# A feed-forward's products with half of the layer stack put between them, and its weights kept split in DRAM

## The reference, cut to what matters

```python
x = x + _L0_attn_a_ref(_layernorm(x), ...)     # stack: DEPTH 4, DIM 64, DFF 256
x = x + _L0_ffn_ref(_layernorm(x), ...)        # I = 1792, w_eff = w * (su @ sv), rank 4
x = x + _L0_attn_b_ref(_layernorm(x), ...)
x = x + _L0_ffn_ref(_layernorm(x), ...)
...
# the stack: project to 64 features, then four times
y = silu(layernorm(h)); y = sconv(y); h = h + y * scl      # sconv: a complex recurrence over 256 tokens
y = layernorm(h); y = silu(y @ w1.T + b1); h = h + (y @ w2.T + b2)
# then layernorm, and a product back to 512 features
```

## Time and profile before

| | us |
|---|---|
| median of 3 runs | 2623.54 (2622.83 to 2625.76) |
| the profiled execution | 2625.9 |
| its span | 2624.2 |
| PE busy | 2521.0 (96%) |
| DVE busy | 1533.0 (58%) |
| ACT busy | 1056.4 (40%) |
| POOL busy | 657.9 (25%) |

### The profile page before, as it was taken

The page is one execution under the profiler, slowest core; times in us unless marked ns, Lnnn a source line. Parts: engine busy times, 40 slices in busy tenths (PEclk is TensorE's granted clock), DMA queues, the critical chain, the costliest instruction groups (busy, mean ns, idle before and its releaser), DMA issues.

```text
span 2624.2 us, 38718 instructions
## 1 busy us (share of the span) xinstructions
PE 2521.0 (96%) x13406; PEld 2141.7 (82%) x13406; DVE 1533.0 (58%) x3579; ACT 1056.4 (40%) x2692; POOL 657.9 (25%) x1156
## 2 busy tenths in 40 slices
PE   3888999999989999999999999999999989999999
PEld 3564788888868888888888888888888868888887
DVE  6776655454446666666666666666666655445443
ACT  2221233333325454544545445545444433333332
POOL 6442000000013343443433434434343310000000
PEclk8767899999989999999999999999999989999999
DMA  3000343222210010000000100001000002323231
GB/s 116 1 0 25 120 169 121 97 97 96 97 42 25 1 41 1 17 25 1 25 18 1 41 1 17 25 1 41 1 17 25 1 29 101 115 87 112 96 112 65
DMA packets 29840, 132.87 MB, mean 51 GB/s; under 512 B 4744, under 2 KB 4872, under 8 KB 29648
## 3 DMA queue, kind: packets, MB, share of 16 engines
q1 hardware_dynamic: 27472, 128.95, 14.5%
q10 hardware_dynamic: 2176, 1.45, 0.2%
HBM read 115.18 MB, written 15.20 MB: 50 GB/s over the span
## 4 chain that ended last, share of the span: by engine, by line
PE 91%; DVE 4%; issue 2%; POOL 1%; ACT 1%; DMA 0%; SPq 0%; DVEq 0%; ACTq 0%; POOLq 0%
PE psum L298 81%; PE psum L1346 3%; PE psum L1321 2%; PE psum L874 1%; PE psum L782 1%; POOL srstd L432 1%; PE psum L883 1%; PE psum L864 1%; PE psum L1301 1%; DVE ln_bn L552 1%; PE psum L773 0%; DVE buf_c L701 0%; PE psum L849 0%; DMA x<-in_x 0%; PE psum L1283 0%
## 5 line engine op out<-in xcount | busy, mean ns | idle before, releaser
L298 PE MATMUL psum<-wkvq_h,axT_h 128*128 128x256 f32 (+1 forms) x1024 | 358.3, 350 | 1.5 <-DVE axT_l L1192 1.5
L298 PE MATMUL psum<-wkvq_h,axT_l 128*128 128x256 f32 (+1 forms) x1024 | 346.8, 339 | 0.0
L298 PE MATMUL psum<-wkvq_l,axT_h 128*128 128x256 f32 (+1 forms) x1024 | 346.3, 338 | 0.0
L1169 POOL TENSOR_SCALAR prob<-prob,rsum 128x128 f32<-128x128 f32 (+1 forms) x512 | 212.7, 428 | 445.0 <-DVE rsum L1261 436.6
L1114 ACT ACTIVATE prob<-biased,nmax 128x128 f32<-128x128 f32 (+1 forms) x512 | 226.2, 443 | 216.2 <-DVE nmax L1254 216.2
L298 PEld LDWEIGHTS psum<-wkvq_h,axT_l 128*128 128x128 f32 x1024 | 195.4, 191 | 21.8
L298 PE MATMUL psum<-wo_h,oT_h 128*128 128x512 f32 x512 | 212.7, 415 | 0.0
L298 PEld LDWEIGHTS psum<-wkvq_h,axT_h 128*128 128x128 f32 x1024 | 195.7, 191 | 17.8 <-issue 1.9
L298 PEld LDWEIGHTS psum<-wkvq_l,axT_h 128*128 128x128 f32 x1024 | 196.1, 191 | 16.1
L298 PE MATMUL psum<-wo_h,oT_l 128*128 128x512 f32 x512 | 201.7, 394 | 0.0
L298 PE MATMUL psum<-wo_l,oT_h 128*128 128x512 f32 x512 | 200.6, 392 | 0.0
(11 more groups left out here) (374 smaller groups left out, 6501.7 us busy)
## 6 DMA issues: line engine op xcount, KB each, us to landing
stage<-weff_dram SPq DMA_DIRECT2D x66, 768.0 KB, 4.2
raw2b<-weff_dram SPq DMA_DIRECT2D x18, 768.0 KB, 4.2
stage<-in_wqkv SPq DMA_DIRECT2D x16, 768.0 KB, 4.3
raw2a<-weff_dram SPq DMA_DIRECT2D x14, 768.0 KB, 4.2
stage<-in_wo SPq DMA_DIRECT2D x16, 512.0 KB, 4.0
stage<-in_ffn_w SPq DMA_DIRECT2D x9, 768.0 KB, 5.5
weff_dram<-stage SPq DMA_DIRECT2D x9, 768.0 KB, 4.0
x<-in_x SPq DMA_DIRECT2D x4, 1024.0 KB, 13.4
```

The costliest lines, as they stand in the source:

```text
L298: ins = pe.matmul(out_ap, stat[a], mov[b], start=start and n == 0, stop=stop and n == last)
L1169: pool.tensor_scalar(prob[:, b, lo:hi], prob[:, b, lo:hi], rsum[:, b, t:t + 1], 1.0, ALU.mult, ALU.mult).then_inc(prob_done, 1)
```

## The change

- **The stack is cut in two.** Blocks 0 and 1 run first, side by side, block 1 later than block 0 by 15 us of a table of step times (`STEP_US`). Block 2 begins one chunk behind the start of the feed-forward, block 3 behind 15 chunks; their steps stand in the lists between the feed-forward's. A `gate`, `up` or `down` is issued in two halves of 6 matmuls, and a stack step can stand between the halves. `merged` puts the chains together by their planned times; a chunk counts as 9.6 us, and a step of blocks 2 and 3 as 1.15 times its table entry, plus 0.8 us if it has work for PE.
- **Buffers and banks.** The stack has two sets of buffers instead of four. Block 0 has two PSUM banks of its own; blocks 1 to 3 share the two banks of `scale` and `fxT` (`AUX`), and PE waits before each use until the last but one user has left (`wait_bank`).
- **The weights are stored in both parts.** In token block 0 they are scaled and split as before, and both parts go to DRAM (`save`), 1.5 MB per chunk. In blocks 1 to 3 and in the second feed-forward, `load` brings both parts back, and nothing is split. Raw weights have two buffers (`stage`), the split ones three (`WSLOTS`). One chunk of the second feed-forward is loaded at the end of the attention, where two raw ones were.
- **The start.** `rstd` of block 0's first norm stands ahead of the last `table` step on POOL.

```diff
+WSLOTS = 3
+
+STEP_US = {"row": 0.6, "xT": 1.6, "proj": 3.6, "h0": 0.6, "cen": 0.8, "sq": 0.5, "var": 0.6, "rstd": 1.6, "rexp": 1.0,
+           "rtr": 0.6, "yn": 0.5, "silu": 0.8, "rot": 0.9, "scan": 1.9, "res": 1.2, "aff": 0.5, "w1": 1.1, "hid": 1.5,
+           "w2": 1.9, "hm": 0.6, "out": 0.5, "xadd": 0.7}
...
-        hres = [sb(f"h{i}", [P, SW], F32, phase1) for i in range(NS)]
...
+        SETS = 2
...
+        hres = [sb1(f"h{i}", [P, SW]) for i in range(SETS)]
+        buf_a, buf_b, buf_c, buf_d, buf_e = ([sb1(f"buf_{n}{i}", [P, SW]) for i in range(SETS)] for n in "abcde")
+        hidden = sb1("hidden", [P, SETS, FC, NG2 * SW])
...
+            d["wgu"] = [place(where if s else head, f"wgu{s}{tag}", [P, 2, 2 * DM], F32R) for s in range(WSLOTS)]
+            d["wdn"] = [place(where if s else head, f"wdn{s}{tag}", [P, 2, DM], F32R) for s in range(WSLOTS)]
...
+        STACK_XT = (0, 1, 1, 0)
+
+
+        LAG = 15.0
+        HALF = 1.6
+        CHUNK = 6 * HALF
...
+        def stack_chain(s, start, busy_from):
+
+            at, chain = start, []
+            for name, n in STACK:
+                chain.append((at, (name, s, n)))
+                at += STEP_US[name] * (1.0 if at < busy_from else 1.15)
+                if at >= busy_from and (name, n) in ON_PE:
+                    at += 0.8
+            return chain, at
...
+                    fresh_next = p == 0 and n + 1 < IC
+                    early, mid, late = [], [], []
+                    if fresh_next:
+                        early, mid = [("scale", n + 1, 0)], [("scale", n + 1, 1), ("sgu", n + 1, 0)]
+                        late = [("scale", n + 1, 2), ("sdn", n + 1, 0)]
                     if n + 2 < NBLK * IC:
-                        order.append(("fetch", n + 2, 0))
-                    elif n + 2 == NBLK * IC and p == 0:
-                        order.append(("kvq", 0, 0))
...
+                    chain += [(t + 2 * HALF, ("up", n, 0)), (t + 3 * HALF, ("up", n, 1))]
+                    chain += [(t + 3 * HALF, e) for e in late]
...
+                        chain += [(t + 4 * HALF, ("down", n - 1, 0)), (t + 5 * HALF, ("down", n - 1, 1))]
...
+        def merged(chains):
+
+
+            order, nxt, holders = [], [0] * len(chains), []
+            while any(k < len(chain) for k, chain in zip(nxt, chains)):
...
+        chain0, ready = stack_chain(0, 0.0, 1e9)
+        first_prep = [(ready + 0.6 * k, e) for k, e in enumerate(
+            [e for step in norm_prep(0, 0) for e in step])]
+        ffn_at = ready + 9.0
...
+        set_up = [(0.5 + 2.5 * k, ("table", k + 1, 0)) for k in range(7)]
+        set_up += [(6.0 + k, ("lr", k, 0)) for k in range(4)]
+        set_up += [(12.0, ("fetch", 0, 0)), (12.0, ("fetch", 1, 0))]
...
+        first_weights = [(ready - 8.0 + 2 * k, e) for k, e in enumerate(
+            [("scale", 0, 0), ("scale", 0, 1), ("sgu", 0, 0), ("scale", 0, 2), ("sdn", 0, 0)])]
+        order1 = merged([chain0, stack_chain(1, LAG, ffn_at)[0], set_up, norms, first_weights, first_prep,
+                         ffn_chain(0, ffn_at, [("kvq", 0, 0)]),
+                         stack_chain(2, ffn_at + CHUNK, 0.0)[0],
+                         stack_chain(3, ffn_at + (IC + 1) * CHUNK, 0.0)[0]])
+        order3 = [("load", 1, 1)] + prep_steps(0) + merged([ffn_chain(1, 0.0, [])])
...
+        GATE, UP, DOWN, AUX = 0, 1, 2, (6, 7)
+        OWN = (2, 3)
...
+        def wait_bank(e):
+
+            first = aux_at[e]
+            for n in range(first, first + (NG2 if e[1] == "w1" else 1)):
+                if n < 2:
+                    continue
+                p, what, a, b = aux_use[n - 2]
+                if what in ("scale", "fxT"):
+                    pe.wait_ge(aux_free, aux_freed[p, what, a, b])
+                elif what == "w1":
+                    pe.wait_ge(stk_act[a], ON_ACT["hid", b, FC - 1])
+                else:
+                    left = {"xT": ("xlo", b), "proj": ("h0", b), "cen": ("cenc", b), "var": ("eps", b), "rtr": ("yn", b),
...
+        def save(n):
+
+            sp.wait_ge(gu_lo, n + 1)
+            sp.dma_start(weff_gu[n], F1["wgu"][n % WSLOTS][:].bitcast(F32)).then_inc(gu_out[n % WSLOTS], 16)
+            sp.wait_ge(dn_lo, n + 1)
+            sp.dma_start(weff_dn[n], F1["wdn"][n % WSLOTS][:].bitcast(F32)).then_inc(dn_out[n % WSLOTS], 16)
...
+            for out_sem, in_sem, used, src, key in ((gu_out, gu_in, up_mm, weff_gu, "wgu"),
+                                                    (dn_out, dn_in, dn_mm, weff_dn, "wdn")):
+                if p == 0 and T == 1:
+                    sp.wait_ge(out_sem[i % WSLOTS], 16 * (i // WSLOTS + 1))
+                if p == 0 and n - WSLOTS < IC:
+                    sp.wait_ge(out_sem[r], 16 * ((n - WSLOTS) // WSLOTS + 1))
+                if n >= WSLOTS:
+                    sp.wait_ge(used, chunk(p, n - WSLOTS) + 1)
+                elif p == 1 and n == 0:
+                    sp.wait_ge(wo_lo, 2 * KVH)
+                sp.dma_start(FB[p][key][r][:].bitcast(F32), src[i]).then_inc(in_sem[r], 16)
...
-        def act_weights(p, what, n):
...
+        def act_weights(what, n):
+            raw, r = stage[:, n % 2, :], n % WSLOTS
+            act.wait_ge(aux_free, aux_freed[0, "scale", n, 1 if what == "sgu" else 2])
+            if what == "sgu":
+                if n >= WSLOTS:
+                    act.wait_ge(up_mm, n - WSLOTS + 1)
+                    act.wait_ge(gu_out[r], 16 * (n // WSLOTS))
+                act.activation(F1["wgu"][r][:, 0, :], raw[:, 0:2 * DM], ACT.Copy).then_inc(gu_hi, 1)
...
+                    dve.wait_ge(gu_hi, a + 1)
+                    w = F1["wgu"][a % WSLOTS]
+                    dve.tensor_tensor(w[:, 1, :], stage[:, a % 2, 0:2 * DM], w[:, 0, :].bitcast(F32),
                                       ALU.subtract).then_inc(gu_lo, 1)
...
+                    ins = mm3(psum[:, bank, :], pairs, start=(b == 0), stop=(b == 1))
+                    if b == 1:
+                        ins.then_inc(gate_mm if what == "gate" else up_mm, 1)
...
+                if what == "load":
+                    load(1, a)
```

More of the change, by code:

```diff
@@ L232, in ffn_steps @@
-                    order += follow[0] + [("gate", n, 0)] + follow[1] + [("up", n, 0)] + follow[2]
-                    if n:
-                        order.append(("down", n - 1, 0))
-                    if ahead:
-                        order += ahead.pop(0)
-                for rest in ahead:
-                    order += rest
-            return order + [("down", NBLK * IC - 1, 0)]
-        set_up = []
-        for k in range(6):
-            set_up.append([("table", k + 1, 0), ("ln", (0, TPB + 2 * k), 2)] + ([("inv", 0, 1 + k // 2)] if k % 2 else []))
@@ L467, in act_ffn @@
                 if what in ("sgu", "sdn"):
-                    act_weights(p, what, a)
-                elif what == "gate":
+                    act_weights(what, a)
+                elif what == "gate" and b == 1:
                     g = chunk(p, a)
```

484 lines of the change are left out of this document (249 added, 235 removed).

## The result

| | before | after |
|---|---|---|
| median, us | 2623.18 (2622.30 to 2625.76, 4 runs) | 2772.63 (2764.93 to 2781.52, 4 runs) |
| ratio | 1 | 1.057, 95% interval 1.054 to 1.060 |
| the profiled execution's span | 2624.2 | 2763.4 |
| first `gate` starts | 274.5 | 207.4 |
| first feed-forward, first `gate` to the start of the last additions to `x` | 478.2 | 684.8 |

What follows compares the result with a forecast made beforehand. Bound: in front the chain of dependent steps of four blocks, in the first feed-forward a full PE. -89.5 + 69.6 + 44.2 + 25.4 + 5 - 3.0 = +51.7 on 2625.9, 2677.6; median 2675 us, range 2595 to 2715.

Steps and rivals of the forecast that it cites:

- PE's work: First feed-forward: work of the moved blocks 2 and 3 plus block 1's `out`, added to a full PE, +69.6 us.
- the sum: Whole kernel: all terms added, +51.7 us on the profiled 2625.9, median 2675; range 2640 to 2715, chance 0.62.
- the clock: Fresh chunks of the first feed-forward: PE's granted clock falls where its work is broken up, +5 us (0 to 60).
- the front: Stack ahead of the first `gate`: with two blocks, 28 us a layer, first `gate` at 185 instead of 274.5, -89.5 us.
- the waits: First feed-forward: PE waits for stack steps queued on DVE, +44.2 us in fresh chunks and +25.4 in the others.
- The second feed-forward: Its start: first rows no longer wait for the split of the first chunk, -3.0 us.
- DMA: Loads of the feed-forwards: the doubled weight traffic fits and costs 0.
- (a): Rival for the whole kernel: the plan holds, 14 us of waits, -25 us, 2598; chance 0.23.
- (b): Rival for the whole kernel: half-way, waits of 23 us instead of 70, 2624, within 0.2%; chance 0.05.
- (d): Rival for the loads: doubled loads land late and hold PE in 98 chunks by 0.2 us, 2695; chance 0.03.
- (c): Rival for the fresh chunks: cold, with the clock at 0.6 there, 2735; chance 0.07.
- The signs: First `gate` at 176 to 198 us, PE waits 50 to 90, token block 0 205 long, its clock above 0.85.

Runs made afterwards that it cites:

- experiment 6: The changed kernel with the next token block's norm and transposes one chunk earlier in both feed-forwards: 2774.35 us, ratio 1.056.
- Experiment 3: The changed kernel with PE alone doing blocks 2 and 3's products and transposes, on constants and input tokens, their other steps left out: 2650.11 us, ratio 1.011.
- experiment 4: Two variants of the changed kernel: first, DVE's three low-part subtractions one place later, 2727.21 us; second, DVE's weights' work cut to 16 columns, 2743.33 us.
- experiment 5: The changed kernel with blocks 2 and 3's steps that have PE work planned 1.4 us apart more instead of 0.8: 2781.33 us, ratio 1.060.

## Why the prediction went wrong

The direction held and its reason too: PE's work comes back in full, and waits come on top. The step that failed worst is the sum's +5 for the clock, with its reason that slow matmuls fill the waits: it measured 38.9. Two more terms were mis-sized, the front (28 us a layer, where 32.5 came) and the waits (69.6, where 91.6 came). The three are 33.9, 22.4 and 22.0 us of the 87.5 by which the profiled execution missed the sum.

**The front: -89.5 forecast, -67.1 measured.** The first `rot` came at 49.31, as walked. What failed is 28 us a layer. It was 32.5: (177.75 - 49.31) / 3.95. Block 0's four stretches, first from `rot` to `rot` and the last from `rot` to `out`, in the changed kernel:

```profile
49.31:82.45 33.14, 19.23 (x78) 14.16 (x78) 16.74 (x37) 5.54 (x11) 8.86 (x9) 0.65 0.01 4
82.45:118.24 35.79, 19.96 (x64) 13.21 (x64) 19.44 (x47) 5.16 (x10) 13.29 (x15) 0.60 0.00 0
118.24:146.94 28.70, 15.20 (x64) 10.08 (x64) 14.41 (x32) 5.16 (x10) 10.13 (x12) 0.74 0.00 1
146.94:177.75 30.81, 18.61 (x72) 13.21 (x73) 14.62 (x32) 5.61 (x10) 9.02 (x10) 0.67 0.00 0
```

and the last two in the kernel of experiment 6, whose front is the same, instruction by instruction:

```profile
120.33:154.37 34.04, 22.18 (x64) 14.80 (x64) 14.45 (x32) 5.15 (x10) 10.12 (x12) 0.50 0.00 1
154.37:189.04 34.67, 23.84 (x73) 16.56 (x73) 14.62 (x32) 5.61 (x10) 9.01 (x10) 0.50 0.00 0
```

Three things are in it. At a clock of 0.74 a plain layer (the third stretch) takes 28.7, near the walk's 28. At 0.50 it takes 34.0 where the walk gave 31.5, so the walk's cold end was too low by 2.5. And the second stretch has 47 DVE instructions instead of 32, the statistics of the tiles of blocks 2 and 3: it took 35.8 at 0.60 in both kernels, and the walk left them out of the layers. The first and the last stretch have 78 and 72 rows on PE instead of 64; how much of their length that is, no run separates. I had also carried over the 0.73 of four blocks side by side to two, which leave PE more idle; 0.66 came. Last, from the first `out` to the first `gate` it took 29.6 instead of 25.

**PE's work: +69.6 forecast, 76.2 measured.** Experiment 3 gives 65.9 for the two blocks where I took 66. The rest is block 1's `out` (3.6 taken) and a clock a little under full even without waits.

**The waits: +69.6 forecast, 91.6 measured.** Those that were walked in the fresh chunks came as walked: `h0` 3.1 forecast and 3.09, `w1` 3.5 and 3.54, the longest `cen` 5.9 and 6.37, a `rtr` behind a late `rexp` 2.9 and up to 3.83. By kind, `h0`, the norms, `cen` and `w1` of token block 0 sum to 43.9 us, against the 44.2 forecast. But PE idles 57.1 us there, and the other 13.2 were not walked: `scale` waits for banks that it now shares with the stack (5.0), block 1's `out` for `x` (4.6), a late transpose (1.8) and block 2's own transposes (1.8). Behind 453.57 us, where I had put 25, PE idles 34.5 us, 3.2 of them for the two other late transposes; which of the `rtr`, `w1` and `cen` there I walked too short I didn't follow further.

**The clock: +5 forecast, 38.9 measured.** This is the largest miss, and it was in my bound (0 to 60) but not in my sum. I had reasoned that slow products fill the waits, and took a clock of 0.75 over the fresh chunks, which made 15.2 us of a chunk instead of 14.6. The clock was better than that, 0.85 over token block 0, and a chunk still took 17.6 us: 13.5 of busy PE (189.12 / 14), which is 11.5 at full clock where I had 11.4, and 4.1 of waits, next to each other and not one inside the other. Experiment 3 shows it directly: 2546 rows of PE in 554 us at 0.99 with few waits, in 593 at 0.93 with many. Taking waits away gave clock back, but at no fixed rate: 13.5 us for 28.9 in the first kernel of experiment 4, 3.9 for 20.6 in the second. The Trainium skill (TensorE: Matmul & The Clock Gate, "Part 1: The HAM clock gate") says that activity releases the throttle, and I had written that by it the upper end is the nearer one; the runs agree (38.9 on a bound of 0 to 60), and I should have weighted my middle by it.

**The second feed-forward: -3.0 forecast, -0.3 measured** for everything behind the first feed-forward. The start did gain: from the attention's last product to the first `gate` 7.9 us instead of 11.2. The attention, its list unchanged, took about 1 us less. But 4.4 are lost again to the late transposes of experiment 6. I read the lists for what was removed there and not for what the new order put ahead of a `gate`.

**DMA: 0, right.** The chain of waits has 396 products of the second feed-forward without a break, 8.19 us for every 36, as in the earlier trace rows, with twice the bytes per chunk:

```profile
2525.47 90.04 PE psum L404 x396
```

**The rivals.** (a), that the plan holds, and (b), half-way, are refuted by the size of the waits, 91.6 us against 14 and 23; experiment 5 adds that a looser plan has as many. (In (a) I took 25.5 us as the lower bound of a layer where my walk had 24.3, which moves (a) by 5 us and nothing else.) (d) is refuted by the chain row above. (c), a clock of 0.6 in the fresh chunks, didn't come either: it was 0.85. It named the term that I had too small, and I gave it 0.07; but its reason, a much colder clock, was wrong as well. The sum by measured terms is -67.1 + 76.2 + 91.6 + 38.9 - 0.3 = +139.3, against 139.2 between the spans; the 0.1 is rounding.

**The signs.** The first `gate` at 207.4 us is outside my 176 to 198, the waits of 91.6 just outside 50 to 90, under the names I gave. Token block 0 took 246 us and not 205. The last chunks take 8.2 us as said, and the clock over block 0 is at the limit I set, 0.85.

**What I should have compared first** is what the moved blocks cost where they stood. My own numbers had it: with 28 us a layer the front was to shrink by 89.5, and 69.6 of work to come back, so the whole promise was 20 us, against waits that the walk of the fresh chunks alone already put above 40. Measured, the promise was 4 us.

## What to carry to other kernels

Before you move work from a stage that isn't full to an engine that is, measure what it costs where it stands, by leaving it out: here 70 us for two of four interleaved chains, against 66 us of PE's pure work at the new place. Then look at the queue of the engine that feeds it: here most of PE's waits came from stack steps queued on DVE behind the feed-forward's. Where that engine stands waiting within a step (1.4 us of 4.05 on DVE here), try the part behind the wait one place later, which brought 45 us of the 149. And don't count on slow products to hide the waits: here the waits came with slower clock on top of their length, 38.9 us for 77.8 of waits, 13.5 for 28.9, and only 3.9 for 20.6.

## What was new about the hardware

The same instructions in front ran at different clocks in different profiled executions: first `gate` between 207.4 us at 0.66 and 219.2 at 0.57, with the clock at 0.74 and 0.67 or at 0.50 in the same layers. That is most of the spread of the changed kernel's runs, 2765 to 2782 us if they differ as the profiles do, and means that one profile places this front only within 12 us. What makes the clock differ stays open.

Idle products raised the clock (0.74 to 0.86 with 88 of them) and gained at best 2 us of 2623, which is within the measurement.

`rexp` on DVE took 1.35 us while POOL added the bias to `x` and 0.29 with POOL idle:

```profile
129.10 1.26 POOL L572 TENSOR_TENSOR x<-x,bout_sb 128x512 f32<-128x512 f32 x1
129.16 1.35 DVE L816 COPY buf_c<-srstd 128x256 f32<-128x256 f32 x1 [1.13 <-POOL srstd L559]
...
134.20 0.29 DVE L816 COPY buf_c<-srstd 128x256 f32<-128x256 f32 x1 [1.13 <-POOL srstd L559]
```

That is the range of the earlier trace rows. The Trainium skill (SBUF — State Buffer, "SBUF: two separate sides") says that DVE and GpSimd share one pair of ports; the rows agree. They agree in the kernel before too, with one exception. Copies that began together with POOL's L437 took 0.81 us and with its L445 1.35, ending just behind it, while those under POOL's `rstd` (L432) alone took 0.29, though that instruction lasts about 1 us:

```profile
94.90 1.13 POOL L432 TENSOR_TENSOR srstd<-svar,mneg_half 128x4 f32<-128x4 f32 x1 [1.58 <-DVE svar L697]
95.08 0.29 DVE L701 COPY buf_c<-srstd 128x256 f32<-128x256 f32 x1
96.00 0.72 POOL L437 TENSOR_TENSOR buf_b<-buf_e,sinT 128x256 f32<-128x256 f32 x1
96.06 0.81 DVE L701 COPY buf_c<-srstd 128x256 f32<-128x256 f32 x1 [0.69 <-POOL srstd L432]
```

In the first feed-forward of the changed kernel 18 such copies have a median of 0.29 us, so the 0.3 of the prediction was right there; the longest took 1.37.
